# A dense layer of eight experts: routing of the next five tiles put inside the products, and activations kept in SBUF across two stage borders

## The reference, cut to what matters

```
x = x + L0_gnn(layernorm(x))     # attention over edges, at its end: sums @ Wo
x = x + L0_ffn(layernorm(x))     # router picks 2 of 6 experts for each row
x = x + L1_gnn(layernorm(x))     # 4 heads: softmax(leaky_relu(al + ar)) mixes them
x = x + L1_ffn(layernorm(x))     # 8 experts, all used, weighted by a softmax
...
def L1_ffn(x):                   # xn, one row
    w = softmax(x @ Wr + br)                        # 8 gates
    h = relu(bn1(x @ W1[e] + b1[e]))                # 256 -> 256, for each e
    h = relu(bn2(h @ W2[e] + b2[e]))                # 256 -> 256
    y = h @ Wo[e] + bo[e]                           # 256 -> 256
    return sum_e w[e] * y[e]
```

## Time and profile before

| | |
|---|---|
| median of 3 runs | 4035.67 us (4034.86 to 4044.26) |
| profiled execution, its own time | 4025.21 us |
| its span, first to last instruction | 4023.7 us |
| granted TensorE clock, mean | 0.881 of full speed |
| PE, DVE, ACT, POOL busy | 76%, 58%, 25%, 49% |
| ffn0 | 1458.0 to 1801.0 us |
| ffn1, routing part | 2293.6 to 2362.2 us |
| ffn1, products part | 2362.2 to 2916.4 us |
| next stage begins | 2921.4 us |

### The profile page before, as it was taken

The page is one execution under the profiler, slowest core; times in us unless marked ns, Lnnn a source line. Parts: engine busy times, 40 slices in busy tenths (PEclk is TensorE's granted clock), DMA queues, the critical chain, the costliest instruction groups (busy, mean ns, idle before and its releaser), DMA issues. The chain is left out here.

```text
span 4023.7 us, 51038 instructions
## 1 busy us (share of the span) xinstructions
PE 3059.4 (76%) x15611; PEld 2533.3 (63%) x15612; DVE 2335.1 (58%) x3854; ACT 1022.6 (25%) x1960; POOL 1979.6 (49%) x1783
## 2 busy tenths in 40 slices
PE   4446666666666555866999689999979995999698
PEld 2235555555555443645888667777758884888586
DVE  8557777777777644437999641111146666334433
ACT  1111111111111121221555433333335552000222
POOL 4567777777777535444760188888400000011333
PEclk8678888888888876987999879999989998999899
DMA  3568888888788674433974574566323542454433
GB/s 103 164 191 230 230 231 230 230 230 230 230 230 230 186 271 142 68 73 79 227 204 191 189 110 14 13 13 7 0 87 118 159 129 99 157 176 168 125 65 51
DMA packets 317791, 591.67 MB, mean 147 GB/s; under 512 B 100508, under 2 KB 221600, under 8 KB 308736
## 3 DMA queue, kind: packets, MB, share of 16 engines
q0 software_dynamic: 160880, 301.94, 35.8%
q1 hardware_dynamic: 137552, 235.63, 17.4%
q10 hardware_dynamic: 19264, 52.97, 4.2%
HBM read 428.73 MB, written 164.27 MB: 147 GB/s over the span
## 5 line engine op out<-in xcount | busy, mean ns | idle before, releaser
L2155 POOL DMA_INDIRECT gnn_got<-kv,gnn_index x928 | 877.3, 945 | 296.3 <-issue 286.9
L2214 PE MATMUL gnn_p_out<-gnn_got,gnn_ident 128*128 128x264 f32 x1856 | 584.7, 482 | 0.0
L2214 PEld LDWEIGHTS gnn_p_out<-gnn_got,gnn_ident 128*128 128x128 f32 x1856 | 444.8, 246 | 97.0
L2196 PE MATMUL gnn_p_stage<-scratch,gnn_scaled 128*128 x236 | 102.4, 522 | 459.1 <-issue 459.1
L2238 DVE TENSOR_TENSOR gnn_prod<-gnn_got,gnn_p_stage 128x2048 f32<-128x2048 f32 x116 | 265.4, 2288 | 195.2 <-DMA gnn_got<-kv,gnn_index 195.1
L2196 PEld LDWEIGHTS gnn_p_stage<-scratch,gnn_scaled 128*128 128x128 f32 x236 | 40.7, 216 | 506.8 <-issue 506.8
L2540 POOL DMA_INDIRECT weight_table<-cell_of,cell_at x192 | 304.4, 1585 | 74.0 <-issue 47.1
L2540 POOL DMA_INDIRECT count_table<-cell_of,cell_at x192 | 303.1, 1578 | 71.6 <-issue 54.7
L2707 PE MATMUL tables_p_pair<-tables_spread,tables_hot 128*128 128x100 f32 x2816 | 321.1, 277 | 2.6 <-DVE tables_spread L2679 2.6
L2707 PEld LDWEIGHTS tables_p_pair<-tables_spread,tables_hot 128*128 128x128 f32 x2816 | 319.3, 194 | 3.9 <-issue 3.7
L799 DVE SCALAR_TENSOR_TENSOR ffn_acc<-ffn_pC,ffn_gates,ffn_acc 128x256 f32<-128x256 f32 x200 | 88.9, 480 | 394.6 <-PE ffn_pC L643 394.6
(11 more groups left out here) (447 smaller groups left out, 5265.5 us busy)
## 6 DMA issues: line engine op xcount, KB each, us to landing
slabs<-weight_table SPq DMA_DIRECT2D x25, 1600.0 KB, 7.8
weight_table<-tables_weight_slab SPq DMA_DIRECT2D x11, 3200.0 KB, 10.2
count_table<-tables_count_row SPq DMA_DIRECT2D x11, 3200.0 KB, 16.7
gnn_cell<-count_table ACTq DMA_DIRECT2D x50, 576.0 KB, 3.8
state<-gnn_out SPq DMA_DIRECT2D x116, 136.0 KB, 3.5
ffn_xs<-by_expert SPq DMA_DIRECT2D x60, 260.0 KB, 3.3
gnn_got<-kv,gnn_index POOLq DMA_INDIRECT x928, 3.8
gnn_cell<-count_table ACTq DMA_DIRECT2D x25, 448.0 KB, 3.4
```

What stands on the lines that cost most here:

```text
L2155: pool.indirect_dma_start(out=got[k][:, r, :], out_offset=None, in_=kv_dram, in_offset=rows_at(index[k][:, r:r + 1])).then_inc(gathered[k] ...
L2214: nc.tensor.matmul(p_out[k][:, 0:MSG], ident[:], got[k][:, r, MSG:2 * MSG], start=(r == 0), stop=False)
```

## The change

1. **ffn1 is pipelined by groups.** `moe_phase` becomes `dense_moe_phase`. Only group 0 is mixed, normalized, turned and routed ahead of the products. For group g+1 the same is done inside the products of group g: DVE mixes after expert 0's combination, normalizes after expert 1's, and makes the gates after expert 6's; PE turns one tile after each of the six layers of experts 3 to 5 (five turns), and multiplies it with the router's matrix one layer later; ACT copies each turned tile once, to `all_xT`, and takes the root after expert 2's second layer and the exponentials after expert 7's first.
2. **Mixed rows stay in SBUF** in the two buffers `x`; the store to and the loads from `mixed_dram` are gone. `x[g % 2]` is filled again once the base of its group has been added.
3. **Weights** are all issued at the start, expert by expert, behind the constants and ahead of the second group's rows, and PE waits for each expert's own.
4. **The loops over groups are written out**; no hardware loop is left in the stage.
5. **Wo's rows stay in SBUF.** `wo` writes its 25 tiles into a tile `x` that ffn0 then uses. The constants and weights of ffn0 (27 loads) are issued during wo as `ahead` loads, behind wo's own. ffn0 waits for none of them, and stores its starting rows at once.

```diff
@@ dense_moe_phase, SP
+                for e in range(Ex):
+                    for to, of in ((wa, w1), (wb, w2), (wc, w3)):
+                        sp.dma_start(to[:, e], of[e].rearrange("(k p) n -> p k n", p=P)).then_inc(weights_loaded[e], 16)
+                    if e == 0:
+                        sp.dma_start(bc[:], b3).then_inc(bias_loaded, 16)
+                sp.dma_start(x[1][:], rows(x_dram, 1, GROUP * P)).then_inc(row_loaded[1], 16)
                 for g in range(GROUPS):
-                    sp.wait_ge(x_mixed, g + 1)
-                    sp.dma_start(rows(mixed_dram, g, GROUP * P), x2[g % 2][:]).then_inc(mixed_stored, 16)
-                    for to, of in weight_loads[g::GROUPS]:
-                        sp.dma_start(to, of).then_inc(weights_loaded, 16)
+                    sp.wait_ge(base_added, BANKS * (g + 1))
                     if g + 2 < GROUPS:
+                        sp.dma_start(x[g % 2][:], rows(x_dram, g + 2, GROUP * P)).then_inc(row_loaded[g + 2], 16)
+                    sp.wait_ge(combined, OUT * (g + 1))
+                    sp.dma_start(rows(out_dram, g, GROUP * P), acc[:]).then_inc(stored, 16)
@@ ACT
+                for g in range(GROUPS):
+                    for e in range(Ex):
+                        for layer in range(2):
+                            hidden(g, e, layer)
+                            step = (e - ROUTED_FROM) * 2 + layer
+                            if g + 1 < GROUPS:
+                                if (e, layer) == (SCALED_AT + 1, 1):
+                                    deviation(g + 1)
+                                if 0 <= step < GROUP:
+                                    copy_turned((g + 1) * GROUP + step)
+                                if (e, layer) == (CHOSEN_AT + 1, 0):
+                                    exponentials(g + 1)
@@ PE
+                def turn(i):
+                    if i % GROUP == 0:
+                        pe.wait_ge(xn_ready, i // GROUP + 1)
...
+                    for k in range(2):
+                        last = nc.tensor.transpose(turned_in(i)[:, k * P:(k + 1) * P], xn[:, i % GROUP, k * P:(k + 1) * P], ident[:])
+                    last.then_inc(turned, 1)
+                def route(i):
+                    pe.wait_ge(xT_ready, i + 1)
+                    for k in range(2):
+                        last = nc.tensor.matmul(pR[:, i % GROUP * Ex:(i % GROUP + 1) * Ex], all_xT[:, k, i * P:(i + 1) * P],
+                                                rw[:, k, :], start=(k == 0), stop=(k == 1))
...
+                for t in range(GROUP):
+                    turn(t)
+                for t in range(GROUP):
+                    route(t)
+                pe.wait_ge(bias_loaded, 16)
                 for g in range(GROUPS):
                     for e in range(Ex):
+                        if g == 0:
+                            pe.wait_ge(weights_loaded[e], 48)
+                        for layer in range(2):
+                            products(g, e, layer)
+                            step = (e - ROUTED_FROM) * 2 + layer
+                            if g + 1 < GROUPS:
+                                if 0 < step <= GROUP:
+                                    route((g + 1) * GROUP + step - 1)
+                                if 0 <= step < GROUP:
+                                    turn((g + 1) * GROUP + step)
                         if e == 0:
+                            base(g)
+                        outputs(g, e)
@@ DVE
+                mix(0)
+                norm(0)
+                dve.wait_ge(const_loaded, 16 * len(loads))
+                fold_features()
+                choose(0)
                 for g in range(GROUPS):
+                    add_base(g)
                     for e in range(Ex):
+                        combine(g, e)
+                        if g + 1 < GROUPS:
+                            if e == MIXED_AT:
+                                mix(g + 1)
+                            if e == SCALED_AT:
+                                norm(g + 1)
+                            if e == CHOSEN_AT:
+                                choose(g + 1)
@@ build_program
-        projection_phase(nc, "wo", ident, None, [a["L0_gnn_Wo"]], [xs[1]], res_dram=xs[0],
-                         normalize=lambda s, loaded: own_rows(nc, s, loaded, state, place, natural))
...
+                kept, loads = first_experts(nc, a, early)
+                projection_phase(nc, "wo", ident, None, [a["L0_gnn_Wo"]], [], res_dram=xs[0], rows_to=kept[0], ahead=loads,
+                                 normalize=lambda s, loaded: own_rows(nc, s, loaded, state, place, natural))
+                ffn0(nc, a, kept, xs[2], by_expert, (zeros, late_rows))
```

More of the change, by code:

```diff
@@ L333, with dense_moe_phase @@
 MIX = 4
-def moe_phase(nc, name, ident_dram, left, right, x_dram, mixed_dram, out_dram, router, gate, w1, hidden_act, w2, w3, b3,
-              beside, inner_norm=None):
+def dense_moe_phase(nc, name, ident_dram, left, right, x_dram, out_dram, router, w1, hidden_act, w2, w3, b3, beside):
     Ex, _, H = w1.shape
     MB = H // P
-    deep = w2 is not None
-    KC = 2 if deep else MB
     halves = [(0, 3), (3, GROUP)]
-    routed = len(router) == 4
+    banks = [(0, 2), (2, 4), (4, 5)]
+    BANKS = len(banks)
+    OUT = Ex * BANKS
+    HID = Ex * 2 * 2 * MB
+    TURN = 256
+    MIXED_AT, SCALED_AT, ROUTED_FROM, CHOSEN_AT = 0, 1, 3, 6
     with ExitStack() as ctx:
@@ L548, in _ @@
[L548 to L566 removed]
+                deviation(0)
@@ new lines, in base @@
+                def base(g):
+                    pe.wait_ge(gates_ready, g + 1)
+                    if g:
+                        pe.wait_ge(combined, OUT * g)
+                    for t in range(GROUP):
+                        last = nc.tensor.transpose(pC[0:Ex, t * P:(t + 1) * P], gates[:, g * GROUP + t, :], ident[:])
+                    last.then_inc(gT_turned, 1)
+                    pe.wait_ge(gT_ready, g + 1)
+                    for t in range(GROUP):
+                        last = nc.tensor.matmul(pC[:, t * F:(t + 1) * F], gT[:, t * P:(t + 1) * P], bc[:], start=True, stop=True)
+                    last.then_inc(base_ready, 1)
@@ L1084, in _ @@
                 sp.wait_ge(all_added, 1)
[L1085 to L1087 removed]
+                if not kept:
+                    sp.wait_ge(weights_loaded, 16 * len(weights))
+                    for e in range(Ex):
+                        sp.wait_ge(late_loaded[e], 16)
                 if clear:
@@ L1561, in ffn1 @@
+def ffn1(nc, a, left, right, x, out, beside):
     p = "L1_ffn_"
-    moe_phase(nc, "ffn1", a["ident"], left, right, x, mixed, out, (a[p + "Wr"], a[p + "br"]), "softmax", a[p + "W1"],
-              [(ACT.Relu, *(a[p + n + str(i)] for n in ("b", "g", "be", "m", "v"))) for i in (1, 2)],
-              a[p + "W2"], a[p + "Wo"], a[p + "bo"], beside)
+    dense_moe_phase(nc, "ffn1", a["ident"], left, right, x, out, (a[p + "Wr"], a[p + "br"]), a[p + "W1"],
+                    [(ACT.Relu, *(a[p + n + str(i)] for n in ("b", "g", "be", "m", "v"))) for i in (1, 2)],
+                    a[p + "W2"], a[p + "Wo"], a[p + "bo"], beside)
```

563 lines of the change are left out of this document (224 added, 339 removed).

## The result

The changed kernel takes 3990.09 us (median of 6 runs, 3984.65 to 4000.83), the kernel before 4038.76 in the same set (6 runs, 4034.86 to 4044.26): ratio 0.9885, interval 0.9869 to 0.9901. The profiled execution of the changed kernel took 3989.85 us (span 3988.3), that of before 4025.21: there the difference is only 35.4 us.

A forecast was written before the change was run, and what follows sets the result against it. ffn1's products were taken as bound by PE, with POOL a close second bound; 48.1 - 14.2 + 8 - 1 = 40.9 us off the median of 4035.67 gave 3995 us, range 3982 to 4012.

The forecast's parts named there:

- First product at 20.5 us, 48.1 saved: Start of ffn1: with only group 0 routed ahead, the first product comes 20.5 us in instead of 68.6.
- Additions to PE 14.2: ffn1's products: 20 inserted tiles at 0.71 us each (turn 0.25, router products 0.46) cost PE 14.2 us.
- A: Rival: additions to PE are dearer, total 4008, or 4032 with 1 us more per step; at full, with E, 0.05.
- B: Rival: PE's clock falls in experts 3 to 5 and the kernel is slower, 4150; B or another loss 0.03.
- E: Rival: nothing won, PE waits 10 us once a group for inputs, 4035; E or A at full 0.05.
- POOL the floor: End of ffn1: POOL ends at 2877.4, PE near 2882.5, so PE could win at most 5 us more.
- rival C: POOL ends ffn1: losing 15 us beside DVE's moved operations and denser loads, total 4005; C or D together 0.08.
- The sign that was named for being wrong here: End of ffn1: POOL's last add behind PE's last product would have shown the forecast wrong.
- wo and ffn0, 8 - 1 = 7: Border of wo and ffn0: 8 us gained by earlier first statistics, 1 us lost to loads beside wo's gathers.
- the 10.5 us between the profiled execution and the median: Offset of the kernel before: median 4035.67 against profiled 4025.21, carried unchanged into the forecast time.
- the POOL floor with wo's best case: Range's lower edge: about 3984, and 2 for the runs' spread, giving 3982.

The follow-up runs named there:

- all routing ahead: On 16 rounds: mixed rows of all five groups kept in SBUF, but all routing done ahead of the products; 4284.6 us, ratio 1.0005 to before.
- three times the transposes: On 16 rounds: each of the 20 turns among the products issues its two transposes three times; 4244.3 us, ratio 0.9920 to before.
- 16 rounds: Changed kernel with 16 instead of 13 rounds of POOL's table additions issued in the tables stage; 3979.9 us, ratio 0.9876 to before.
- the second set: Set of follow-up runs on a chip on which the stages ahead of wo took 1626 us instead of 1401.
- wo's rows only: Kernel before with only the new wo and ffn0 (rows kept in SBUF, loads ahead) and the old dense layer; 4017.1 us, ratio 0.9976.
- late router products: On 16 rounds: group 0's router products come behind expert 0's first layer; 3980.3 us, ratio 0.9880 to before.
- two sum buffers: On late router products: base's parts moved among products in groups 1 to 4, plus second sum buffer; 3968.8 us, ratio 0.9853, fastest measured.
- dense layer only: Changed kernel's dense layer alone, with wo and ffn0 as in the kernel before; 3993.4 us, ratio 0.9913.
- rows without weights: Changed kernel with the 21 expert weight loads issued in ffn0 again, only rows and six constants ahead; 3986.2 us, ratio 0.9897.

## Why the prediction was right, point by point

The forecast was 3995 with 3982 to 4012; measured 3990. In gain it was 40.9 us; measured 46 by the times and 35.4 between the two profiles. Its mechanism held, one step of it failed, and the number came out near in part by luck. The steps:

- **First product at 20.5 us, 48.1 saved.** Measured 19.7 and 48.8. The chain held; the kernel with all routing ahead shows from the other side that this place is the gain.
- **Additions to PE 14.2.** The periods give 0.84 + 1.24 + 1.07 = 3.15 us a group, 12.6 in four. A turn took 0.26 (2377.24 to 2377.50), as priced; the router's products took 0.36 a tile (2376.88 to 2377.24) instead of 0.46. Expert 0 took 1.1 us more over five groups, within its scatter, so the products part is 13.7 longer. No gap in PE at the additions, the clock 1.00 in the window shown: rivals A, B and E are gone, B with three times the transposes as well.
- **POOL the floor, "PE could win at most 5 us more before POOL ends the stage".** This is the step that failed. PE ended 587.6 us into the stage (588.9 forecast), and with 0.6 us to the store and the 4.4 of store and border the stage would have ended 592.6 in, as it does with 16 rounds; it ended 597.8 in. The floor was put at the end of POOL's last issue (583.8 in). It lies 12.7 us behind that end: 6.6 until the last addition had landed, 5.0 of POOL's DRAIN, 1.0 of barrier. So there was no room of 5 us left but a loss of 5.2. That is rival C in kind, by another route than the one given for it: POOL lost almost no time in its own work (585.1 us from the stage's start to its last issue's end, 583.8 before). The sign that was named for being wrong here, POOL's last add behind PE's last product, did not show (2875.4 against 2877.8), and POOL ended the stage all the same. The landing and the DRAIN could be read in the trace of the kernel before, where they ended at 2888.7 and not at 2877.4. In ffn1 the terms then give 33.9 + 0.7 (first product) + 0.5 (additions) - 5.2 = 29.9, which is what the profiles differ by.
- **wo and ffn0, 8 - 1 = 7.** The border gave 8.5, wo's last sum came 0.4 later; over the profiled executions without the second set, whose chip is slower in these stages, wo and ffn0 take 400.7 us in the old form (399.6, 402.5, 400.1) and 392.9 in the new one (six executions, 392.0 to 393.7): 7.8. The weights ahead are not part of it.
- **The sum against the profile.** I carried the 10.5 us between the profiled execution and the median along as a constant. It was not one: the old ffn1 alone took 627.7, 631.1 and 637.7 us, by waits for transfers that the change takes away. With the means, the gain is 34.2 + 7.8 = 42.0; the times say 46 (40 to 53), and 41.5 (35 to 48) for the kernel without the weights ahead (0.9897). So the sum of the means lies inside both intervals; whether something beyond these waits makes up the rest of the 46 is open. The mis-sized floor made the forecast gain 5 us too large, and the profile of before, a fast draw, made it some 4 us too small. They met near the measured time, and that is luck. The base moved as well: the median of before was 4035.67 over three runs and 4038.76 over six.
- **The range.** Its lower edge does not follow from its terms: the POOL floor with wo's best case is 48.1 - 14.2 + 5 + 9.1 = 48.0 us of gain, 3988, and 3986 with the spread, not 3982. The measured time lies in either range.

## What to carry to other kernels

A stage that ends in a wait for scatters ends when the last one has landed and the issuing engine has closed its part (here 6.6 and 5.0 us behind its last instruction). Put an engine's end there before calling it off the path. Work that is routed among the products of a full PE costs its own time at the full clock and nothing more, if its inputs are ready ahead; take it from the stretch where PE is cold. And where a stage waits for transfers, one profile is one draw: profile the kernel before twice before carrying its offset into a forecast.

## What the runs showed of the hardware

- Behind its last indirect addition POOL was not free: the wait for the landing ended 6.6 us after the instruction's end in the changed kernel (6.2 in the kernel before), and its DRAIN took 5.0 us more (5.0 before too, 3.5 with 16 rounds).
- The last store of 640 KB landed 3.3 us after its issue where POOL's additions were over (before, wo's rows only, 16 rounds, late router products, two sum buffers), and 6.4, 5.2 and 6.9 where they were in flight (changed, dense layer only, rows without weights).
- The same program at two borders of one execution (two sum buffers) got a granted clock of 0.58 and 1.00 for 4 us, after PE had done five small transposes and ten products over 8 rows and had waited for nothing; 20 output products took 4.89 us and 4.48 there. What differed is not shown. Among full products neither router products nor transposes did this (1.00 over 55 and 60 us).
- The first 16 products of ffn1 took 6.6 us in the changed kernel, 6.2 in the kernel before and 7.6 in the fastest one, instead of 4.47; in the latter the granted clock was 0.50 and then 0.78 there. An earlier start pays this once, as a later one does.
- A store of 640 KB issued behind 6 MB of weight loads landed 13.9 us later; such stores of the sums land in 6.6 in the changed kernel (median).
- Between two chips the stages with gathers differed by 16% (1401 and 1626 us ahead of wo, 228 and 194 GB/s in their middle), the tables and all stages behind ffn1 by less than 2 us each on average; wo, ffn0 and xt took up to 11, 11 and 13 us more.
